# One chunk of the dt, B, C projection taken out of its place, expert outputs carried over a batch's end, and batch 0's jobs re-placed

## What is computed

```python
x = x + attn(cond(x))                      # per batch element
x = x + ffn(cond2(x))
# cond:  x W^T + b + 2 (x A_j) B_j          adapter j from an index
# attn:  u, gate = split(h W_in^T)          2048 channels each
#        u = silu(causal_conv4(u) + conv_b)
#        dt, B, C = rmsnorm of u Wx^T       64 + 16 + 16 columns
#        delta = softplus(dt Wdt^T + bias)
#        state = exp(delta A) state + delta u B     16 states a channel, over 256 steps
#        y = (sum_n C state + D u) * silu(gate);  out = y W_out^T
# ffn:   softmax gate, top 2 of 8 experts of rank 64, over cond2(x)
```

## Time and profile before

| | us |
|---|---|
| median of three runs (lowest, highest) | 2556.78 (2555.78, 2558.4) |
| profiled execution | 2555.34 |
| its span, first to last instruction | 2553.6 |
| VectorE busy | 2234.1 (87%) |
| GpSimd busy | 2121.3 (83%) |
| TensorE matmul busy | 2273.3 (89%) |
| ScalarE busy | 1620.3 (63%) |

### The profile page before, as it was taken

One profiled execution on the slowest core, in us unless ns is written; L12 is line 12 of the kernel. 1 busy time (PEld: TensorE's weight loads), 2 busy tenths in 40 slices (PEclk: granted clock), 3 DMA queues, 4 the chain that ended last, 5 costly groups with the idle time before them and its releaser, 6 DMA issues.

```text
span 2553.6 us, 30492 instructions
## 1 busy us (share of the span) xinstructions
PE 2273.3 (89%) x10128; PEld 1918.1 (75%) x10128; DVE 2234.1 (87%) x2098; ACT 1620.3 (63%) x3768; POOL 2121.3 (83%) x1092
## 2 busy tenths in 40 slices
PE   7978898899879997999889997899978978787878
PEld 6867786688768886788768886788867766666767
DVE  1369797899989998999989998999989999999892
ACT  1367566776577766775667665776667765776550
POOL 0088787899889998999979998999979998999880
PEclk9989999899899998999999998999989998888989
DMA  6363443444345433544445433544426332432332
GB/s 209 125 212 100 115 142 119 151 142 139 119 171 155 140 133 105 197 149 140 125 142 168 148 126 116 177 160 136 135 70 215 116 108 91 169 120 90 116 104 89
DMA packets 132250, 350.05 MB, mean 137 GB/s; under 512 B 38573, under 2 KB 43181, under 8 KB 130621
## 3 DMA queue, kind: packets, MB, share of 16 engines
q1 hardware_dynamic: 109326, 296.19, 36.1%
q10 hardware_dynamic: 22768, 51.93, 6.0%
HBM read 337.04 MB, written 11.02 MB: 136 GB/s over the span
## 4 chain that ended last, share of the span: by engine, by line
PE 51%; DVE 22%; ACT 12%; issue 7%; POOL 7%; ACTq 1%; DMA 0%; SPq 0%; DVEq 0%; POOLq 0%
DVE scan L1241 12%; PE late L666 11%; PE ubank L584 10%; PE ubank L613 9%; ACT scan L1076 7%; DVE st L1253 5%; PE gbank L566 5%; POOL st L1464 3%; POOL st L1472 2%; PE scan L584 2%; PE small L640 2%; DVE ubank L1222 2%; PE gbank L630 2%; PE scan L566 1%; ACT ubank L937 1%
## 5 line engine op out<-in xcount | busy, mean ns | idle before, releaser
L1464 POOL TENSOR_TENSOR st<-w_sb,bc 128x1024 f32<-128x1024 f32 x512 | 1198.1, 2355 | 163.5 <-PE gbank L630 150.2
L1241 DVE TENSOR_TENSOR_SCAN scan<-scan,st 128x1024 f32<-128x1024 f32 x512 | 1156.5, 2285 | 40.1 <-POOL st L1464 22.7
L1076 ACT ACTIVATE scan<-delta,A_sb 128x255 f32<-128x255 f32 x2048 | 846.2, 459 | 0.0
L1472 POOL TENSOR_TENSOR st<-st 128x1024 f32<-128x1024 f32 x256 | 603.1, 2356 | 73.1 <-DVE st L1253 63.0
L584 PE MATMUL ubank<-h,wt 128*128 128x256 f32 x1712 | 445.2, 419 | 130.5 <-ACT qg L1155 125.7
L613 PE MATMUL ubank<-h,wt 128*128 128x256 f32 x2048 | 481.6, 390 | 41.5 <-ACT qg L1155 36.3
L584 PEld LDWEIGHTS ubank<-h,wt 128*128 128x128 f32 x1712 | 360.1, 213 | 208.4 <-ACT qg L1155 150.6
L1073 ACT ACTIVATE scan<-iota 128x4 f32<-128x4 f32 x512 | 86.8, 170 | 655.0 <-DVE st L1253 631.6
L613 PEld LDWEIGHTS ubank<-h,wt 128*128 128x128 f32 x2048 | 400.4, 196 | 103.7 <-ACT qg L1155 40.9
L1253 DVE TENSOR_TENSOR st<-scan,bc 128x1024 f32<-128x1024 f32 x384 | 453.7, 1207 | 0.0
L666 PE MATMUL late<-yg,wt 128*128 128x256 f32 x1792 | 410.5, 388 | 32.6 <-DVE x L1278 29.6
(11 more groups left out here) (217 smaller groups left out, 2253.8 us busy)
## 6 DMA issues: line engine op xcount, KB each, us to landing
wt<-in_W_in SPq DMA_DIRECT2D x256, 512.0 KB, 3.6
wt<-in_W_out SPq DMA_DIRECT2D x128, 512.0 KB, 3.4
wt<-in_cond_W SPq DMA_DIRECT2D x64, 512.0 KB, 3.6
bc<-bc_rows ACTq DMA_DIRECT2D x64, 512.0 KB, 6.6
wt<-G_tiles SPq DMA_DIRECT2D x32, 512.0 KB, 3.6
wt<-in_ffn_B SPq DMA_DIRECT2D x26, 512.0 KB, 3.4
xb<-in_x SPq DMA_DIRECT2D x8, 1024.0 KB, 5.6
x<-in_x ACTq DMA_DIRECT2D x28, 256.0 KB, 3.9
```

Of the source, the lines that this page charges most:

```text
L1076: last = fn(t[:, k, 1:T], delta[:, c, 1:T], ACT.Exp, scale=A_sb[:, col:col + 1])
L1241: v_.tensor_tensor_scan(Tps[q % 2][:, :], Tps[q % 2][:, :], x_, 0.0, ALU.mult, ALU.add).then_inc(scan_done, 1)
L1464: tt(st[:, n % ST_RING, :, :], w_sb[:, i % 2:i % 2 + 1, :].to_broadcast([P, NQ, T]), bc[:, 0, q * NQ:(q + 1) * NQ, :], ALU.mult).then_inc( ...
L1472: tt(st[:, n % ST_RING, :, :], st[:, n % ST_RING, :, :], st[:, (n - 1) % ST_RING, :, :], ALU.add).then_inc(add_done, 1)
```

## The change

It moves work; no arithmetic changes.

- xp becomes the small job of chunk 12: fifteen products (fourteen in batch 0) before `sum_states`, the rest after `ubank_free` and ahead of u. Before, all sixteen stood at the chunk's end, behind u and gate.
- A 1 goes from chunk 11 to 13, wb 1 from 13 to 14, B 0 from 14 to 15, B 1 from 15 to the next batch's chunk 0. B 2 becomes two single outputs: Bs 4 and 5 stand in chunk 15 and the next chunk 0, Bs 6 and 7 in its chunks 1 and 2. The last batch keeps its order.
- Conditioning tiles 0 to 7 stand in chunks 3, 5, 7, 8, 9, 9, 11, 11, with 6 in bank `late` in chunk 11; before in 1, 3, 5, 6, 7, 8, 9, 9.
- In batch 0, two u chunks are made in chunks 1 to 4 and in 11, one in 5 to 10. g 0 to 4 stand in chunks 6 to 10, bias in 11, b2 in 13, g 5 and 6 in 14 and 15, g 7 in chunk 16; before g 0 to 6 in 6 to 12, g 7, b2, bias in 13 to 15.
- ScalarE takes `pro_cond(1, 4)` and `(1, 5)` before `decay(1, 0)` and `(1, 1)`, and 6 and 7 before and after `decay(1, 2)`. The first x2 loads go from chunk 16 to 17, and the later stores and loads of x2 by one chunk or two.

```diff
     if b == 0:
         if c == 0:
             return []
-        if c <= 5:
+        if c <= 4:
             return [NC + 2 * (c - 1), NC + 2 * c - 1]
-        if c <= 11:
-            return [NC + 10 + (c - 6)]
+        if c <= 10:
+            return [NC + 8 + (c - 5)]
+        if c == 11:
+            return [NC + 14, NC + 15]
     return [i + LEAD]
...
-        return {13: ("g", 0, 7), 14: ("b2", 0, 0), 15: ("bias", 0, 0)}.get(c)
-    f = b - 1
+        return {13: ("b2", 0, 0), 14: ("g", 0, 5), 15: ("g", 0, 6)}.get(c)
+    f, j = b - 1, b + 2
     if c == 0:
-        return ("B", f - 1, 2) if f else None
+        return ("B", f - 1, 1) if f else ("g", 0, 7)
     if c <= 8:
         return ("wout", f, c - 1)
     if c == 9:
         return ("la2", f, 0)
-    if c in (10, 11):
-        return ("A", f, c - 10)
-    if c in (12, 13):
-        return ("wb", f, c - 12)
-    return ("B", f, c - 14)
+    if c == 10:
+        return ("A", f, 0)
+    if b == LAST:
+        return {11: ("A", f, 1), 12: ("wb", f, 0), 13: ("wb", f, 1), 14: ("B", f, 0), 15: ("B", f, 1)}[c]
+    if c == 11:
+        return ("cond", j, 6) if j < B else None
+    return {12: ("wb", f, 0), 13: ("A", f, 1), 14: ("wb", f, 1), 15: ("B", f, 0)}[c]
...
-    if c == 13 and b < LAST:
-        return ("ms", b + 1, 0)
-    if c in (14, 15) and b < LAST:
-        return ("dt", b + 1, c - 13)
+    if b < LAST and c >= 12:
+        return {12: ("xp", b + 1, 0), 13: ("ms", b + 1, 0), 14: ("dt", b + 1, 1), 15: ("dt", b + 1, 2)}[c]
     if b == 0:
         if c <= 5:
             return ("dt", 0, c + 2)
-        return ("g", 0, c - 6) if c <= 12 else None
+        return ("g", 0, c - 6) if c <= 10 else ("bias", 0, 0)
     f, j = b - 1, b + 2
     if c <= 4:
         return ("dt", b, c + 3)
-    if c in (6, 9) and j < B:
-        return ("cond", j, {6: 3, 9: 6}[c])
+    if c == 9 and j < B:
+        return ("cond", j, 4)
     if c in (10, 11):
         return (("lg", "wT")[c - 10], f, 0)
-    if c in (14, 15):
+    if b == LAST and c in (14, 15):
...
-    if c == 0:
-        return ("la", 3, 0) if f == 0 else ("Bs", f - 1, 7)
-    if j < B and c in (1, 3, 5, 7, 8, 9):
-        return ("cond", j, {1: 0, 3: 1, 5: 2, 7: 4, 8: 5, 9: 7}[c])
+    if f and c <= 2:
+        return ("Bs", f - 1, 5 + c)
+    if f == 0 and c == 1:
+        return ("la", 3, 0)
+    if j < B and c in (3, 5, 7, 8, 9, 11):
+        return ("cond", j, {3: 0, 5: 1, 7: 2, 8: 3, 9: 5, 11: 7}[c])
     if c == 14 and b + 3 < B:
         return ("la", b + 3, 0)
     if c == 15 and b < LAST:
-        return ("Bs", f, 6)
+        return ("Bs", f, 4)
...
-    if b < LAST:
-        if c == 12:
-            return ("xp", b + 1, 0)
-        if c == 13:
-            return ("dt", b + 1, 0)
-    return None
+    return ("dt", b + 1, 0) if b < LAST and c == 13 else None
...
-            return late if NC <= v < NC + 10 and v % 2 else ubank
+            return late if NC <= v < 2 * NC and v % 2 and (v < NC + 8 or v == 2 * NC - 1) else ubank
...
-            def x_proj(job):
+            def x_proj(job, cs):
                 b = job[1]
-                pe.wait_ge(u_done, NC * (b + 1))
-                for c in range(NC):
+                pe.wait_ge(u_done, NC * b + cs[-1] + 1)
+                for c in cs:
                     n = TILE_NO[("wx", b, c // 8)]
                     if c % 8 == 0:
                         pe.wait_ge(*loaded(n))
                     last = mm(home(job)[0:RX, 0:T], wx_tile(n)[:, c % 8, :], u_sb[:, (NC * b + c) % U_RING, :],
                               start=(c == 0), stop=(c == NC - 1))
-                last.then_inc(done_inc(job), 1)
+                if cs[-1] == NC - 1:
+                    last.then_inc(done_inc(job), 1)
...
-                    x_proj(job)
+                    x_proj(job, range(NC - 1 if i % NC == 12 and i >= NC else NC - 2))
...
                 ubank_free(i)
+                if small_job(i) and small_job(i)[0] == "xp":
+                    x_proj(small_job(i), range(NC - 1 if i >= NC else NC - 2, NC))
                 for v in us:
                     if v % NC == 0:
                         h0_ready(v // NC)
+                    if v == 2 * NC - 1:
+                        pe.wait_ge(*emptied(("g", 0, 4)))
...
-                    if job == ("g", 0, 7):
-                        pe.wait_ge(*emptied(("g", 0, 6)))
+                    if job == ("b2", 0, 0):
+                        pe.wait_ge(*emptied(("g", 0, 4)))
+                        for v in u_chunks(11):
+                            pe.wait_ge(u_done, v + 1)
...
-                    if k < KH - 1:
-                        for v in u_chunks(5):
+                    if k < 5:
+                        for v in u_chunks(4):
...
+                    if i == 1:
+                        pro_cond(1, 6)
+                if i == NC + 1:
                     for k in range(PAIRS):
                         load_x2(0, k)
+                if b >= 2 and c in (1, 2, 4):
+                    for k in {1: [0], 2: [1, 2], 4: [3]}[c]:
+                        load_x2(b - 1, k)
                 if c == 15 and b < LAST:
                     for q in range(3):
                         load_B(b + 1, q)
                 decay(i, 2)
+                if i == 1:
+                    pro_cond(1, 7)
...
-                    for m in range(4, KH):
-                        pro_cond(1, m)
+                    pro_cond(1, 4)
                 if c == 13 and b < LAST:
                     store_rows(b + 1)
-                if b and c == 15:
+                if b >= 2 and c in (0, 1, 3):
+                    for k in {0: [0], 1: [1, 2], 3: [3]}[c]:
+                        store_out(b - 2, k)
+                if b == LAST and c == 15:
                     store_out(b - 1, 0)
-                if b >= 2 and c == 0:
-                    load_x2(b - 1, 0)
-                    store_out(b - 2, 1)
-                if b >= 2 and c == 1:
-                    load_x2(b - 1, 1)
-                    store_out(b - 2, 2)
-                    store_out(b - 2, 3)
-                if b >= 2 and c == 2:
-                    load_x2(b - 1, 2)
-                    load_x2(b - 1, 3)
+                    store_out(b - 1, 3)
                 if i + 1 < CHUNKS:
                     decay(i + 1, 0)
                     if c == 15:
                         load_C(b + 1, 2)
+                if i == 0:
+                    pro_cond(1, 5)
...
-                        dve.wait_ge(G_st, 16 * KH)
+                        dve.wait_ge(G_st, 16 * 5)
+                        dve.wait_ge(bias_st, 32 * GR)
                     if i == NC + 1:
-                        dve.wait_ge(*made(("bias", 0, 0)))
+                        dve.wait_ge(*made(("g", 0, 7)))
```

36 lines of the change are left out of this document (20 added, 16 removed).

## The result

| | before | after |
|---|---|---|
| median of the runs, us | 2556.28 (2551.16 to 2558.40) | 2523.03 (2520.20 to 2525.12) |
| profiled execution, us | 2555.34 | 2525.12 |
| span of the profiled execution, us | 2553.6 | 2523.3 |
| mean granted TensorE clock | 0.945 | 0.959 |

The ratio is 0.9872, with a 95% interval of 0.9854 to 0.989: 33 us, 1.3%. The span is 30.3 us shorter.

A forecast was written before the change was run, and what follows sets the result against it. VectorE's queue was taken as the bound, GpSimd close behind. Terms -8.1 - 12.1 + 1.5 - 7.4 - 4.3 - 8.5 + 6.6 = -32.3 took 2555.34 to 2523.0; with 1.4 for the median, 2524.5 us, range 2506 to 2543.

The forecast's parts named there:

- A: Batch 0's chunks 0 to 3: one evacuation, not four, precedes the decay chunk 1's first scan needs; -8.1 us.
- B: Batch 0's chunk 6: TensorE's 6.58 idle goes as u chunks leave bank `late` after chunk 4; -12.1 us.
- C: Batch 0's chunks 11 and 12: the u chunk comes back in 11, its three taps in 12; +1.5 us.
- D: Batch 0's chunks 13 to 15: x_proj no longer ahead of ms; chunk 13 -6.3, 14 -0.9, 15 -0.2; -7.4 us.
- E: Chunks 16 and 17: bias stores go to chunk 12, x2 loads to 17; -5.5 and +1.2, together -4.3 us.
- F: Batches 1 to 5: chunks 8 and 13 gain, 11 and 14 lose; -1.7 us per batch, -8.5 in all.
- G: The rest: Bs in chunks 2 and 3 +3.3, batch 6's chunk 13 +3.0, batch 7 +0.3; +6.6 us.
- (1): Rival, batches 1 to 5: the gap of chunk 11 costs no clock; -14 over five batches, 2510 us; chance 0.12.
- (2): Rival: batches gain nothing, F = +5, A and E at their low ends; 2543 us; chance 0.15.
- (3): Rival: TensorE stays at 1.2 GHz from wT through ms, so the kernel is slower, 2625 us; chance 0.04.
- (4): Rival: batch 0 does not gain, loads come late for the earlier TensorE; A and B nil, 2545 us; chance 0.04.

The follow-up runs named there:

- pro_back: The changed kernel with ScalarE's four evacuations of batch 1's conditioning rows 4 to 7 in a row again in chunk 0: 2532.02 us, ratio 0.9908.
- u_back: The changed kernel with batch 1's u chunks dealt out to batch 0's chunks as before the change: 2538.58 us, ratio 0.9929.
- fill_11: The changed kernel with ten idle products filling TensorE's gap ahead of the transposed weights' product in chunk 11 of batches 1 to 5: 2510.26 us, ratio 0.9821.
- experts_back: The changed kernel with batches 1 to 7's expert and conditioning jobs back in the chunks where the kernel before had them: 2493.21 us, ratio 0.9758.
- fill_13: The changed kernel with six idle products between the states' sum and the u chunk in chunk 13 of batches 1 to 5: 2509.13 us, ratio 0.9815.

## Why the prediction was right, step by step

The forecast was 2524.5, and 2523.0 was measured; the span moved by -30.3 for a predicted -32.3. The terms, by chunk lengths of the two profiled executions:

| term | predicted | measured |
|---|---|---|
| A, chunks 0 to 3 | -8.1 | -7.2 |
| B, chunk 6 | -12.1 | -12.4 |
| C, chunk 12 of batch 0 | +1.5 | +1.4 |
| D, chunks 13 to 15 of batch 0 | -7.4 | -6.5 |
| E, chunks 16 and 17 | -4.3 | -4.5 |
| F, batches 1 to 5 | -8.5 | -7.2 |
| G, Bs, batches 6 and 7 | +6.6 | +5.0 |
| not foreseen: first scan later, tail | 0 | +1.0 |
| sum | -32.3 | -30.4 |

The number is closer than the working. The terms miss by up to 1.6 us to either side, and the span came out 2.0 short of the gain forecast. The forecast then put the median 1.4 above the profiled execution, and it lies 2.1 below, since that execution was the slowest of the four; this is luck. The mechanisms of A, B and C were each undone by a run and came back. Chunk 13 of term D, and term E, are read from the traces before and after: no run undid either by itself. What the runs show is the sum: A to E make 29.2 us by the table, and batch 0's part of the change, put in as a whole, 28.

**A.** One evacuation ahead of each decay, as said; VectorE waits 0.76 for chunk 1's first scan and 1.89 for its fourth, where the prediction had 2.6 for that one, and chunks 0 and 1 give -7.4 for -6.9. pro_back puts the wait back. The estimate of -1.2 for chunks 2 and 3 was wrong, they gave +0.2.

**B and C.** Right, and u_back returned both (12.1 and -1.4).

**D.** Chunk 13 is -6.3, as worked out. Chunk 14 was to gain 0.9 and gained nothing: dt 0 stands behind the u product there, as said, and that product took 6.32 us. Why one can't count on that number is in the last section.

**E.** Chunk 16 is 17.23 for a predicted 17.2. The open point was what four x2 loads cost in chunk 17, 0.4 each or the 4.29 of the earlier trace rows again:

```profile
453.68 1.93 ACTq L1016 DMA_DIRECT2D x<-in_x  x4
```

0.48 each, and chunk 17 grew by 0.94 (predicted 1.2): the choice and its reason, that the eight stores ahead of the loads had gone, fit. No run took the stores back, so the reason is read and not tested. In chunk 12, where the stores stand now, nobody waited for them.

**F.** The mechanism was right in each chunk of batch 3. Chunk 8 is exact. In chunk 11 TensorE's idle was 5.12 (predicted 5.4), its loss behind it, wT included, 2.83 (2.8), conditioning 7 made 19.8 in (19.2); +1.9 for +1.3. In chunk 12 the state sum is made 14.51 in (14.5), and GpSimd's slack covered it: it waits 4.64 there, and VectorE waits for nothing. In 13 the mean square is made 12.83 in (13.0), chunk 13 is 20.78 (21.1). In 14 dt 0 is made 7.78 in (7.2): +2.4 for +1.7. Chunk 14 was under-priced because its slow stretch was: 3.12 lost by the u product where 2.5 was taken. Chunk 11 was not, its loss was right: wT started 0.16 later than in the kernel before, and from wT to the end of conditioning 7 TensorE needs 5.54 at full rate (fill_11) where the forecast's 19.2 leaves about 5.2. Chunk 13's -4.1 for -3.7 gives part of it back. Per batch, chunks 4 to 15 gave only -0.9, -0.8 and -0.8 in batches 2 to 4, half of the predicted -1.7; the total of -7.2 is near -8.5 because batches 1 and 5 gave -2.3 and -2.4, by a shorter slow stretch in chunk 11 or 14 and, in batch 1, 0.65 in chunk 7. That, too, is luck.

**G.** Bs costs 0.33 in each of two chunks, in five batches; experts_back takes just that away again. Batch 6's chunk 13: TensorE idle 4.00 before A 1 (4.3), which takes 5.41, 21.10 for 21.8. Batch 6's chunk 11, which the earlier trace rows does not list, was 1.48 shorter than before, and it is one of the chunks that differ between kernels with the same order.

**The rivals.** (1), that the gap costs no clock, is refuted by fill_11; its price, 13 us for the place, was right within 1. (2), batches gaining nothing, is nearer than the forecast made it: batches 2 to 4 end within 0.3 us of before once Bs is counted. (3) did not occur: chunk 12, filled with x_proj, has a granted clock of 1.00. (4) did not occur.

**The Trainium skill's rule.** fill_11 and fill_13 measure what the prediction could only weigh: 12.8 and 13.9 us for one gap in each of five batches, 0.5% of the span each. The Trainium skill, "TensorE: Matmul & The Clock Gate", section "What's actually happening", puts the ramp penalty under 1% of a typical span and advises against fitting it to a count. Each of the two agrees with that bound; added they would be 26.7 us, 1.06%, and no run fills both gaps. Not charging them would have made the forecast wrong by 13 us for chunk 11's gap alone, though, against an effect of 33.
